# Second feed-forward product in pairs of token tiles, as seven block products instead of eight

## The reference

```python
x = x + attn(_layernorm(x), w_qkv, w_out)       # 16 heads of 64, causal window of 128
x = x + ffn(_layernorm(x), W1, b1, W2, b2)

def bitlinear(x, W, b):
    w_scale = clip(mean(abs(W)), EPS)
    Wq = clip(round(W / w_scale), -1, 1) * w_scale           # weights -1, 0, 1
    x_scale = clip(max(abs(x), axis=-1), EPS)
    xq = clip(round(x * (127 / x_scale)), -128, 127) * (x_scale / 127)
    return einsum('bnd,hd->bnh', xq, Wq) + b

def ffn(x, W1, b1, W2, b2):                     # W1: 1024 -> 4096, W2: 4096 -> 1024
    h = gelu(bitlinear(x, W1, b1), approximate=False)
    return bitlinear(h, W2, b2)
```

## Time and profile before

| What | Value |
|---|---|
| Median of 3 runs | 1572.35 us |
| The profiled execution, its own time | 1573.67 us |
| Its span, slowest core (core 2) | 1571.9 us |
| Spans of all 8 cores | 1557.0 to 1571.9 us |
| Mean granted TensorE clock by core | 0.988 to 0.993 |
| PE busy | 1489.5 us, 95% |
| DVE busy | 1072.7 us, 68% |
| ACT busy | 797.8 us, 51% |
| POOL busy | 250.2 us, 16% |
| Moved by DMA | 213.74 MB, mean 136 GB/s |

### The profile page before, as it was taken

The page is one execution under the profiler, slowest core; times in us unless marked ns, Lnnn a source line. Parts: engine busy times, 40 slices in busy tenths (PEclk is TensorE's granted clock), DMA queues, the critical chain, the costliest instruction groups (busy, mean ns, idle before and its releaser), DMA issues.

```text
span 1571.9 us, 33942 instructions; the slowest of 8 cores (1557.0 to 1571.9 us)
## 1 busy us (share of the span) xinstructions
PE 1489.5 (95%) x11685; PEld 838.6 (53%) x11748; DVE 1072.7 (68%) x2697; ACT 797.8 (51%) x1836; POOL 250.2 (16%) x199
## 2 busy tenths in 40 slices
PE   3789999999899999989999999999999999999998
PEld 3556677667566676644444444444444444444443
DVE  2468888888788999776666666666566666656653
ACT  3667877777677777754333333333333333333321
POOL 0000012222223333103010101101010110101000
PEclk9799999999999999999999999999999999999999
DMA  9768878677776676444424334343443424334332
GB/s 296 212 157 230 236 215 235 202 225 216 179 201 166 189 197 191 107 113 99 113 61 89 93 77 105 63 111 69 82 101 74 108 61 102 80 80 101 73 76 54
DMA packets 275113, 213.74 MB, mean 136 GB/s; under 512 B 237184, under 2 KB 237312, under 8 KB 274944
## 3 DMA queue, kind: packets, MB, share of 16 engines
q1 hardware_dynamic: 270336, 194.79, 49.3%
q0 software_dynamic: 4608, 16.78, 2.8%
HBM read 120.29 MB, written 33.55 MB: 98 GB/s over the span
## 4 chain that ended last, share of the span: by engine, by line
PE 76%; DVE 12%; issue 6%; DMA 2%; SPq 2%; ACT 1%; POOL 0%; DVEq 0%; ACTq 0%; POOLq 0%
PE f L204 30%; PE av L204 29%; PE sc L204 15%; DVE msc L473 4%; DVE xr L240 2%; SPq L190 2%; DVE lnc L331 1%; DMA wst<-wqkv 1%; DMA xlnT<-xln 1%; DVE PT L253 1%; DVE tern L227 1%; PE tA L209 1%; ACT probs L220 1%; PE tB L209 1%; POOL xln L227 0%
## 5 line engine op out<-in xcount | busy, mean ns | idle before, releaser
L204 PE MATMUL av<-W2q,hqT 128*128 128x512 fp8e4 x2048 | 447.2, 379 | 1.7 <-DVE msc L237 1.7
L220 ACT ACTIVATE hbuf<-hb 128x512 f32<-128x512 f32 x256 | 160.3, 629 | 450.5 <-DVE hb L237 450.4
L204 PEld LDWEIGHTS av<-W2q,hqT 128*128 128x128 bf16 x2048 | 200.0, 98 | 243.9 <-issue 2.2
L220 ACT ACTIVATE probs<-msc,cells 128x256 bf16<-128x256 f32 (+1 forms) x512 | 250.8, 491 | 95.7 <-DVE cells L473 95.0
L204 PE MATMUL f<-xlnT,wqkv_sb 128*128 128x128 bf16 x4096 | 258.1, 223 | 20.6 <-DMA xlnT<-xln 8.4
L204 PEld LDWEIGHTS f<-xlnT,wqkv_sb 128*128 128x128 bf16 x4096 | 239.8, 100 | 35.4 <-issue 35.2
L204 PE MATMUL f<-W1q,xlnT 128*128 128x512 fp8e4 x1040 | 235.6, 379 | 0.3 <-DVE hb L237 0.3
L204 PE MATMUL sc<-W1q,xlnT 128*128 128x512 fp8e4 x1008 | 227.8, 379 | 0.0
L473 DVE CUSTOM_DVE_ANT_0 msc<-sc,masks 128x256 f32<-128x256 f32 (+1 forms) x512 | 182.3, 411 | 45.7 <-PE sc L204 41.4
L220 ACT ACTIVATE hq<-hbuf,konst,fhc 128x1024 f16<-128x1024 f32 x128 | 148.3, 1229 | 88.6 <-DVE fhc L225 85.2
L204 PEld LDWEIGHTS f<-W1q,xlnT 128*128 128x128 bf16 x1040 | 101.6, 98 | 122.3 <-issue 0.9
(11 more groups left out here) (87 smaller groups left out, 1390.6 us busy)
## 6 DMA issues: line engine op xcount, KB each, us to landing
stg<-w1t SPq DMA_DIRECT2D x64, 512.0 KB, 7.5
stg<-w2t SPq DMA_DIRECT2D x64, 512.0 KB, 5.3
xr<-xc SPq DMA_DIRECT2D x32, 512.0 KB, 4.9
x1sp<-xr POOLq DMA_DIRECT2D x32, 512.0 KB, 6.3
xr<-x1sp SPq DMA_DIRECT2D x32, 512.0 KB, 4.6
y<-msc SPq DMA_DIRECT2D x31, 512.0 KB, 3.3
wst<-wqkv SPq DMA_DIRECT2D x24, 512.0 KB, 18.7
wst<-wout SPq DMA_DIRECT2D x8, 512.0 KB, 19.8
```

The source lines that it names most:

```text
L204: return op("pe", lambda e: e.matmul(out=out, lhsT=lhsT, rhs=rhs, start=start, stop=stop), waits, sig)
L220: return op("act", lambda e: e.activation(out=out, in_=in_, func=func, **kw), waits)
```

## The change

The hidden rows of two tiles, a = 2p and b = 2p + 1, and the weights W2 are cut into two by two blocks. With A the rows (first index: tile; second: half of the 4096 contraction) and B the weights (half of the contraction by half of the 1024 outputs), the eight block products of a pair become seven (Strassen): M1 = (A11 + A22)(B11 + B22), M2 = (A21 + A22) B11, M3 = A11 (B12 - B22), M4 = A22 (B21 - B11), M5 = (A11 + A12) B22, M6 = (A21 - A11)(B11 + B12), M7 = (A12 - A22)(B21 + B22). A block product is 16 matmuls of 128 x 512. In the code:

- `wsum` forms the five sums of weight blocks X1, X3, X4, X6, X7 once, in fp8, on POOL: 20 instructions of 128 x 2048. X3 and X4 overwrite blocks of W2q. They are put into the last three tiles of attention (X6, X3, X7) and into the start of the feed-forward stage (X4, X1).
- `tq` now transposes into four tiles HT (A11, A12, A21, A22). `asum` forms S1, S6 on DVE and S7, S2, S5 on POOL, bf16, 128 x 2048 each, once for each pair; S2 and S5 overwrite A21 and A12.
- `prod` issues the seven products of a pair into four banks in turn (two of `av`, and `tA`, `tB`); `into` adds each from PSUM into one or two halves of x1: 12 DVE instructions of 128 x 512 for each pair, in place of two of 128 x 1024 (`out`). `store` writes halves (256 KB).
- x1 is loaded twice for a tile: `load_x1` for the input quantization, which is now done in place, and `load_xo` for the sum. `hq` has two buffers and `fhc` four.
- The order is by pairs: `w1_stage(a)`, then `w1_stage(b)` with `unoff(a)` between its first four units, then the seven products, with `unoff(b)` and the input quantization of the next pair beside them.

The core of the diff:

```diff
-            tk["xc", t] = ts("pool", xcb[t % 2], x1r[t % 4], 1.0,
-                             nmean[:, t:t + 1], ALU.mult, ALU.add,
+            x = x1f[t % 2]
+            tk["xc", t] = ts("pool", x, x, 1.0, nmean[:, t:t + 1], ALU.mult,
+                             ALU.add, waits=[tok("x1", t), tok("nmean", t)])
...
+        def asum(p, name):
+            o, a, b, f, w = {
+                "S1": (SX[0], 0, 3, ALU.add, [tok("M1", p - 1)]),
+                "S6": (SX[1], 2, 0, ALU.subtract, [tok("M6", p - 1)]),
+                "S7": (SX[2], 1, 3, ALU.subtract, [tok("M7", p - 1)]),
+                "S2": (HT[2], 2, 3, ALU.add, [tok("S6", p)]),
+                "S5": (HT[1], 1, 0, ALU.add, [tok("S7", p)])}[name]
+            q = "dve" if name in ("S1", "S6") else "pool"
...
+            tk[name, p] = tt(q, o, HT[a], HT[b], f, w + htok(p, a, b))
...
+            tk[name, c] = tk[name] = op(
+                "pool", lambda e: e.tensor_tensor(out=o, in0=a, in1=b, op=f,
+                                                  saturate=False),
...
+            for k in range(16):
+                v = mm(bank[i], a[:, k * 128:(k + 1) * 128], b(k),
+                       k == 0, k == 15, w if k == 0 else (), sig=(k == 15))
...
+        INTO = {"M4": ((1, 0, 1), (0, 0, 1)), "M3": ((0, 1, 1), (1, 1, 1)),
+                "M1": ((0, 0, 1), (1, 1, 1)), "M2": ((1, 0, 1), (1, 1, -1)),
+                "M5": ((0, 1, 1), (0, 0, -1)), "M6": ((1, 1, 1),),
+                "M7": ((0, 0, 1),)}
...
+                tk["out", t, n] = bfree[i] = stt(
+                    x, bank[i], fhc[t % 4][:, c:c + 1], x, ALU.mult, ALU.add,
+                    [tok(name, p), tok("s2", t), tok("xbias", t),
+                     tok("out", t, n)])
...
+            for u in range(8):
+                w1_pe(t, u)
+                pre_gelu(t, u)
+                if u < 4:
+                    if pend:
+                        unoff(t - 1, u)
...
+        for c in range(4):
+            wsum("X4", c)
+        w1_stage(1, True, after_first)
...
+        for c in range(4):
+            wsum("X1", c, [tok("O", lt, 1), tok("AV", nstep - 1),
+                           tok("AT", lt)])
...
+            if not last:
+                w1_stage(a, p == 0, first_sums(p) if p else None)
...
+                if more:
+                    front_pool(a + 2)
+                    front_pool(b + 2)
+                for n in ("S7", "S2", "S5"):
+                    asum(p, n)
+                w1_stage(b, True)
...
+            add_bias(2 * p)
+            add_bias(2 * p + 1)
...
+            for n in MS:
+                prod(p, n)
...
+                into(p, n)
```

More of the change, by code:

```diff
@@ L82, in _build @@
     fqc = [sb("fqc0", 8, F32), sb("fqc1", 8, F32)]
-    fhc = [sb("fhc0", 8, F32), sb("fhc1", 8, F32)]
+    fhc = [sb("fhc%d" % i, 10, F32) for i in range(4)]
     absc = sb("absc", 64, F32)
@@ L1059, in _build @@
                 load_bias(0)
+            if t == nt - 3:
+                wsum("X6", c, [tok("task", n) for n in
+                               range(ntask - 2, ntask)])
             if t == nt - 2:
@@ L1107, in _build, with w1_stage @@
             o_pe(lt, h, av[:, h * 512:(h + 1) * 512], tok("N", lt, 1))
-        for r in range(4):
-            rnd(0, r)
-        for u in range(4):
-            w1_pe(1, u)
-            pre_gelu(1, u)
-            unoff(0, u)
+        def w1_stage(t, pend, mid=None):
+            if pend:
+                for r in range(4):
+                    rnd(t - 1, r)
+            for u in range(8):
+                w1_pe(t, u)
+                pre_gelu(t, u)
+                if u < 4:
+                    if pend:
+                        unoff(t - 1, u)
+                        if u == 3:
+                            for v in range(4):
+                                gelu(t, v)
+                    else:
+                        gelu(t, u)
+                else:
+                    gelu(t, u)
+                if mid is not None:
+                    mid(u)
+                if u % 2 == 1 and u >= 3:
+                    hmax(t, u // 2 - 1)
+            hmax(t, 3)
+            fh(t)
@@ new lines, in first_sums, with mid, after_first @@
+        def first_sums(p):
+            def mid(u):
+                if u == 1:
+                    asum(p, "S1")
+                if u == 3:
+                    asum(p, "S6")
+            return mid
+        def after_first(u):
+            if u == 3:
+                for h in range(2):
+                    resid(lt, h, av[:, h * 512:(h + 1) * 512])
+                ln2_sum(lt)
+                for t in (lt - 1, lt):
+                    ln2_sq(t)
+                spill(lt)
+        for c in range(4):
+            wsum("X4", c)
@@ L1165, in _build @@
-        for half in range(2):
-            out(nt - 1, half)
-        QUEUE["sp"].append(([tok("y", nt - 2), tok("yh", nt - 1, 0),
-                             tok("yh", nt - 1, 1)], None, None, 0))
+        load_xo(0)
+        front_pool(3)
+        front_max(3)
+        front_q(3)
+        xt(3)
+        for c in range(4):
+            wsum("X1", c, [tok("O", lt, 1), tok("AV", nstep - 1),
+                           tok("AT", lt)])
+        np_ = nt // 2
+        bfree += [tok("R", lt, 0), tok("R", lt, 1), tfree[0], tfree[1]]
@@ L1170, in run @@
+        QUEUE["sp"].append(([tok("y", t, n) for t in (nt - 2, nt - 1)
+                             for n in range(2)], None, None, 0))
         def run(q):
```

293 lines of the change are left out of this document (177 added, 116 removed).

## The result

The changed kernel takes 1665.6 us (median of 4 runs, 1658.5 to 1668.0), the kernel before 1573.3 us on the same chip: ratio 1.058, 95% interval 1.055 to 1.062, so 5.8% slower. The profiled execution took 1667.95 us. Executions in which the cores of one die (four of the eight) ran at a lower clock than the others are left out of all medians given here, so that a median can stand a few microseconds off the one that an expectation quotes.

What follows compares the result with a forecast made beforehand. The prediction took PE's matmul count to bound the feed-forward stage; 1518.4 us plus 107, 3, 6.5, 29 and 12 us of losses made 1675.9, less 1.3 for the median, 1674 us, range 1560 to 1725.

Steps and rivals of the forecast that it cites:

- the likeliest case: Feed-forward stage: DVE stopped at POOL's long instructions, so the kernel gets slower, 1620 to 1725 us; chance 65%.
- products, with all else in time: Feed-forward products: 240 matmuls a pair instead of 256 save 55.3 us, leaving 1518.4 us if nothing else ends late.
- attention's last three tiles: End of attention: 12 POOL sums make some 14 DVE instructions wait, 32 us, of which 12 us are left.
- start of the stage, up to the end of pair 0: Feed-forward start: eight more POOL sums, then the first pair's, hold the first three tiles' unoffs; 29 us in all.
- pairs 1 to 13: Steady feed-forward pairs: unoffs wait for POOL and banks are freed late, 8.2 us lost a pair, 107 us.
- pair 14: Next-to-last feed-forward pair: no quantization and POOL is early, so 3 us lost.
- last pair: Last feed-forward pair: nothing hides POOL's sums and additions, so M5 waits 6.5 us for its bank.
- The walk through a pair: One feed-forward pair step by step: unoffs wait under S2, S5 and two bias additions; 60.6 us against 51.8.
- the signs that were named: Trace: POOL sums 4.5 to 4.7 us, even-tile unoffs 2 to 4, pairs 59 to 61, POOL busy about 25%.
- The third rival: Feed-forward pairs: POOL keeps the port until its last addition ends, a pair takes about 64 us, 1750 us; chance 5%.
- the waits are hidden: Feed-forward pairs: DVE's five spare microseconds and four rotating banks swallow the waits, 1530 us; chance 18%.
- The short sums: POOL adds 16-bit and fp8 pairs in 2.24 us, a pair takes 53.0 us, 1564 us; chance 12%.

Runs made afterwards that it cites:

- run 7: Changed kernel with sums, bias additions and quantizations reordered to avoid DVE-POOL meetings, first and last pair's sums on DVE, early unoffs on ACT: 1537.3 us, ratio 0.978.
- run 1: Changed kernel with POOL's sums S7, S2 and S5 cut to 128 columns except in pair 0: 1560.1 us, ratio 0.993 to the kernel before.
- run 9: Run 7's kernel with all X1 sums behind tile 3's quantization and pair 0's sums spread over five units: 1530.5 us, ratio 0.976 to the kernel before.
- run 4: Changed kernel with fp8 sums X4 and X1 put behind the input quantizations of tiles 2 and 3: 1658.4 us, ratio 1.055 to the kernel before.
- run 11: Changed kernel with X4 on whole rows of 2048, its first instruction also waiting for the end of the X7 ahead: 1644.8 us, one execution.
- run 10: Changed kernel with one of four roundings of even tiles moved from ACT to DVE, under POOL's bf16 sums: 1678.8 us, ratio 1.072 to the kernel before.
- run 12: Changed kernel with X4 on whole rows of 2048, its first instruction waiting only for an X7 long past: 1663.2 us, one execution.
- run 8: Changed kernel with the unoffs taking their -1536 from SBUF instead of as an immediate: 1667.4 us, ratio 1.060 to the kernel before.
- run 3: Changed kernel with the unoffs moved from DVE to ACT: 1594.4 us, ratio 1.014 to the kernel before.

## Why the prediction came out

The time was put at 1674 us and came to 1665.6; the likeliest case happened, by its own mechanism, and the sizes of its terms were off in both directions, which is luck in the sum. Term by term, in the profiled execution:

| Term | predicted | measured |
|---|---|---|
| products, with all else in time | 1518.4 | 1518.4 (51.80 us for every pair in run 7, for nearly all in runs 1 and 9) |
| attention's last three tiles | 12 | 23.9 (tile 1 starts at 719.9, 696.0 before) |
| start of the stage, up to the end of pair 0 | 29 | 24.9 |
| pairs 1 to 13 | 107 (8.2 each) | 91 (7.0 each) |
| pair 14 | 3 | 1.4 |
| last pair | 6.5 | 9.9 |

The measured terms sum to 1669.5, against 1667.95.

**Prices.** POOL's 2048-wide sum was taken at 4.66 us, by the row of f32 additions. Undisturbed it takes 4.06 in bf16 and 3.82 in fp8. This is one size that was off in the steady pairs: three sums are 1.8 us shorter, and the pair lost 1.2 less. Another thing that was off is the clock, which was in no term. In nine of the 13 pairs the granted clock falls to the 1.2 GHz level for 3.4 us after PE's waits:

```profile
1308.73 2.50 PE L212 MATMUL f<-W1q,xlnT 128*128 128x512 fp8e4 x8 [2.30 <-DVE hb L245]
1311.02 4.74 PE L212 MATMUL tB<-W2q,HT 128*128 128x512 fp8e4 x16
```

From 1308 to 1313 it is 0.69 on average. Eight matmuls take 1.89 us and sixteen 3.62 otherwise. Half of PE's busy time in the nine stretches is 15 us, an estimate of what this cost. So of the 91 us some 76 are waiting, 5.8 in a pair where 8.2 was predicted, and 15 are the clock. The Trainium skill (GPSIMD Engine Reference, "Performance versus the Vector engine") has 4497 ns for 2048 fp32; it gives no figure for the narrower types, and the trace has both below it. S1 and S6 were taken at 1.6 and take 1.22 when nothing holds them. A half of a product into y was taken at 0.75 and takes 0.745.

**The walk through a pair.** Its order stands. The unoffs' ends were worked out at 23.1, 28.0, 30.6 and 33.3; they came at 20.4, 24.6, 28.8 and 31.3. PE stopped before units 6 and 7 of tile b, and not before unit 5 as well; the first product ended at 31.3 (33.3 predicted), 3.7 us late and not 5.7; and M5 and M6 were late once more, by 0.59 and 1.88 us. The loads of x1 landed at +13.8, later than the 12.5 taken, and S7 began at 16.1 in place of 13.8; so the first unoff met S7's end and not S2, and the shorter sums made up for the rest. Of the signs that were named, the unoffs fit (2.67 us on average in tile a, 0.42 in tile b, over the pairs of the trace); POOL's sums (4.06), the pair (58.8) and POOL's share of the span (32%, not 25) lie outside what was given for them, and PE's waits stand nearly all before matmuls into f (34.7 us, against 2.6 before sc, from 850 to 1480 us).

**Attention's end and the start of the stage.** Here a step failed. The table divides by place, the prediction divided by sums: its 12 us were for the twelve sums X6, X3 and X7, its 29 us for X4, X1 and the first pair. X4 already runs before tile 1 starts, so that 16.63 of the 23.9 us are PE's wait behind the quantization that X4 held, and about 2 more are the lower clock after it (from attention's last 16 matmuls of x with w_out to the first product of tile 1 it is 6.2 us, 4.7 before, where the clock had also fallen for 3.4 us). That leaves some 5 us for the twelve sums (6 by the mean of the cores in run 4) where 12 were taken, and about 43 us for the start where 29 were. Fourteen meetings at 2.3 us were too many or better hidden; and under X4 and X1 the prediction saw only unoffs, each waiting for one sum, where the quantizations of tiles 2 and 3 were held to the end of the run of sums, with PE idle for 16.63 and 7.91 us. The third rival, that POOL keeps the port, held in those places, though not in the pairs, where the earlier trace rows was the right guide. The prediction priced it for all pairs or for none, and did not ask for each run of POOL's instructions which DVE instruction meets it. So the two errors have opposite signs: 41 us were taken for both terms together, and 48.8 came.

**Last pair.** The order of events was right: M5 waits for the bank of M4, behind POOL's sums and bias additions. It was due at +13.8 and starts at +21.8 (the first product of the pair is at 1628.26): 8.0 us late where 6.5 was taken, its own wait of 6.50 on top of M2's lateness of 1.3. What was missing is the other side of the meeting:

```profile
1629.27 6.21 DVE L240 TENSOR_TENSOR SX<-HT,HT 128x2048 bf16<-128x2048 bf16 x2
1630.05 4.34 POOL L240 TENSOR_TENSOR SX<-HT,HT 128x2048 bf16<-128x2048 bf16 x1 [30.50 <-DMA HT<-hq]
1639.94 3.61 PE L212 MATMUL av<-W2q,HT 128*128 128x512 fp8e4 x16 [1.15 <-POOL HT L240]
1650.05 5.85 PE L212 MATMUL av<-W2q,HT 128*128 128x512 fp8e4 x16 [6.50 <-DVE xr L245]
```

S6 asks while S7 runs and ends 1.1 us after it; S2, which needs HT2 back from S6, starts that much later. The Trainium skill (SBUF — State Buffer, "SBUF: two separate sides") counts DVE instructions with two SBUF inputs among those that wait for POOL's lock; here the trace agrees. The 2.5 us that the prediction gave for it, and did not add, went in the right direction; M2 is late by 1.3 for it. That M5's own wait is 6.50 us, the number that was predicted, is chance: the sums were shorter, but S7 began only 1.8 us into the products (1630.05), where the prediction let it begin with them. The 16 matmuls behind the wait take 5.85 us in place of 3.62, which is the rest of the 9.9: PE had stood idle for 6.50 us and came back at a lower clock (0.50 from 1650 to 1654). This part was in no term. After the 2.31 us of idling at 1134.32 there is no such loss, after the 2.30 at 1308.73 there is.

**The rivals.** That the waits are hidden was wrong although DVE's 47 us fit: room in a pair does not help an instruction that must be through at one moment. Run 1 bears out the half of it that DVE has the room (pairs of 51.9 on average once the sums are short), and run 7 the whole pair at 51.80 with all sums in it, once they are placed. The short sums fell too: POOL's sums were priced at 2.24 us there and take 4.06 and 3.82.

## What to carry to other kernels

When work goes to POOL, write down for every POOL instruction which DVE instructions ask while it runs, and which of those are of the kinds that waited here: unoff, quantization, S1 and S6. The `hb` and the halves of products, which read PSUM, and the maxima kept their times (0.75 and 1.21 us). A sum of busy times says nothing about it. The price of a meeting is the rest of the POOL instruction plus what stands behind DVE in its queue, so the cure is order: here the same work on the same engines goes from 1.058 to 1.019 by moving three instructions in POOL's queue. It goes to 0.976 when the pairs are free of meetings and nearly all others are gone too, for which some sums and unoffs at the start and the end also change their engine. Runs of POOL instructions that touch each other need a look of their own: put the DVE instruction that matters ahead of the run, by a wait (run 4), or a pause into it (run 11).

## What was not expected of the hardware

- DVE's quantization (f32 to f16) is shut out of an unbroken run of POOL's fp8 sums, four of them, for 16 to 17 us on every core, while unoffs (f16 to bf16) get in behind each sum of such a run (3.4 us each), and the same f32 to f16 form gets in behind one bf16 sum (at most 4.65 us, run 10). A centring and one fp8 sum that touch are enough: one tile earlier the quantization asks under the centring and is held to the end of the sum of X3 behind it, 4.69 us (656.00 in the changed kernel, 4.68 to 4.71 on the other cores). A pause of 0.14 us in POOL's run ends it (run 11), and the pattern of the sums is not its cause (run 12). Why fp8 sums and bf16 sums differ in this stays open. Which of type, length (3.8 against 4.06 us) or POOL's waits ahead of each bf16 sum decides was not tried, nor whether the factor that the quantization takes from SBUF has a part in it: run 8 put such an operand under bf16 sums only.
- ACT is not held by POOL's sums: its unoff takes 1.13 us beside them (run 3).
- POOL's two-input additions of 2048: 4.06 us in bf16, 3.82 in fp8, where 1024 in f32 take 2.35.
